# Convolution stage of a hybrid kernel: half of the Toeplitz tiles loaded by DMA instead of built by transposes

## The chip, the cores and the metric

One core of a Trainium2 chip. The metric is the device time of one execution of the whole kernel in microseconds (us), lower is better. A fair part of the document is about four engines that work side by side: TensorE (PE; its weight loads are listed as PEld), VectorE (DVE), ScalarE (ACT) and GpSimd (POOL), and about SyncE (SP), which issues most of the loads from DRAM.

## The reference, cut to what matters

```python
# x: (16, 32, 16, 16) f32
def _L0_conv_ref(x, weight_comp, kpe):          # weight_comp (32, 169), kpe (1, 1, 51, 51)
    ...
    weight = weight_comp[:, IDX_MAP].reshape(dim, 1, KS, KS) + kpe      # KS = 51
    pad = KS // 2
    return jax.lax.conv_general_dilated(x, weight, window_strides=(1, 1), padding=[(pad, pad), (pad, pad)],
                                        dimension_numbers=('NCHW', 'OIHW', 'NCHW'), feature_group_count=dim)
```

It is a depthwise convolution: every channel has its own 51x51 filter, which is a coarse per-channel filter (weight_comp, its 169 values spread over the taps) plus one fine filter of positions that all channels share (kpe). An image is 16x16, so only the middle 31x31 taps meet it. The convolution's result is divided by its standard deviation per image and channel and added to x; behind it come a layer norm over channels, an attention over 256 tokens with a mask of spikes, and steps of attention and feed-forward layers that are chosen from the data. All of that is untouched by the change.

## The kernel before, in words

The convolution is done as matmuls with Toeplitz tiles: `toep[:, c, e, x]` has, for channel c, 128 rows (8 image rows of 16 columns) by 24 x 16 f32 (NE = 24, HW = 16); all 32 channels lie in the tile `big`, 128 x 12288 f32. A group of the convolution (cg, eight of them, CG = 8) is four channels; `convolve(j)` (L678) does the groups 2j and 2j + 1 with 32 matmuls.

The tiles are built per block of eight channels (ck = 0 to 3, C8 = 8). `filter_rows` (L374) adds the per-channel weights `wx` and the shared `kx` into `filt` with nine small additions: block 0 on VectorE, blocks 1 to 3 on POOL (L489). `toeplitz(ck)` (L662) transposes windows of `filt` on TensorE, 24 transposes (L675) into six PSUM banks; ACT (L1147) and VectorE (L1403) copy the banks into `big`, by the letters of TOEP (L301), three each for a block in blocks 1 to 3 (four and two in block 0).

The order of TensorE's work is written by hand (L709 to L734): toeplitz 0, means, toeplitz 1, convolve 0, sums of squares (L720), toeplitz 2, a small matmul for the variance (L726), convolve 1, toeplitz 3, to_tokens 0, convolve 2, to_tokens 1, convolve 3, to_tokens 2 and 3. `to_tokens` (L698) transposes scaled groups back (L704), four transposes each. The scaling by the reciprocal deviation is done by ACT (L1153) and VectorE (L1409), four groups each by the letters CDRAIN (L295). On VectorE's queue there stand, behind the copies: the reciprocal (L1424), scalings, the preparations L1433 to L1442 (block-diagonal weights, constants), the step table L1445 to L1453, the last scaling, and then the layer norm, which starts with L1498 (x plus convolution). The step table goes out by two small DMAs (L420, L422).

The loads are issued in this order (sizes in MB of 10^6 bytes): identity 0.066, wx of block 0 0.074, wx of blocks 1 to 3 0.221, xrev 0.524 (x, columns reversed, read by the convolution), constf 0.190, two of attention weights 0.035 and 0.021, xin 0.524 (x as it is, read at L1498), the step masks 0.001, maskc 0.262, gather 0.131, chosen 0.033, spread 0.016, all by SP; kx 0.254 by ACT at the start.

```python
TOEP = "AADADA" + "ADAADA" + "ADADAD" + "ADADAD"
CDRAIN = "AADDADAD"
for ck in (1, 2, 3):                                       # POOL
    filter_rows(ck, pool, nc.gpsimd.tensor_tensor, s_filtP)
```

Of the kernel before, what the change touches and what calls it, by code (L numbers as in the profile page):

```python
# [11 lines left out]
ALU = mybir.AluOpType  # L12
ACT = mybir.ActivationFunctionType
AX = mybir.AxisListType

P = 128
B, C, HW = 16, 32, 16
# [11 lines left out]
C8 = 8  # L29
NCK = C // C8  # L30
NB = 2 * HW - 1
NOPS, NSTEPS, HID = 19, 33, 128
# [5 lines left out]
NONE = 4 * NSTEPS  # L38
CG = C // GB
NV = 8  # L40
# [54 lines left out]
def build(nc, d):  # L95
    with ExitStack() as ctx:
        def sb(name, shape, dt=F32):
            return ctx.enter_context(nc.sbuf_tensor(name, shape, dt))

        def sem(name):  # L100
            return ctx.enter_context(nc.semaphore(name))
# [6 lines left out]
        def part(t, n):  # L108
# [19 lines left out]
        sqc = sb("sqc", [P, C, NH, B])  # L128
        wx = sb("wx", [P, NCK, NQ, HW])
        filt = sb("filt", [P, NCK, NB, HW])  # L130
        big = sb("big", [P, C * NE * HW])
# [112 lines left out]
            "deviation_ready", "rstd_ready"))  # L244
        s_conv, s_convA, s_convD = sem("conv_in_psum"), sem("conv_scaled_by_act"), sem("conv_scaled_by_dve")
        s_lnc, s_lns, s_lnv, s_lnd, s_ln = (sem(n) for n in (
# [44 lines left out]
        NT = NE // 4  # L291
        TBANK = [(0, 1, 5, 7, 6)[n % 5] for n in range(3 * NT)] + [(0, 1, 5, 7)[n % 4] for n in range(NT)]
        STATS = 4
        CBANK = (2, 2, 3, 3, 2, 3, 0, 1)
        CDRAIN = "AADDADAD"  # L295
        TOKENS = (4, 6)
# [3 lines left out]
        WARM = 20  # L300
        TOEP = "AADADA" + "ADAADA" + "ADADAD" + "ADADAD"  # L301
        CONVT = "DD"
# [26 lines left out]
        def count(who, owners):  # L329
            return sum(o == who for o in owners)  # L330
# [71 lines left out]
        def _(sp):  # L402
# [3 lines left out]
            sp.dma_start(flat(xrev[:, :, :, :]).rearrange("p (h n) -> p h n", h=NH),  # L406
                         d["xrev"].rearrange("(h p) n -> p h n", p=P)).then_inc(s_xrev, 16)
            sp.dma_start(constf[:, :], d["constf"]).then_inc(s_cf, 16)
            sp.dma_start(wl1[:, :], d["wl1"]).then_inc(s_wl1, 16)
            sp.dma_start(wl2[:, :], d["wl2"]).then_inc(s_wl2, 16)  # L410
            sp.dma_start(flat(xin[:, :, :, :]).rearrange("p (h n) -> p h n", h=NH),
                         d["xtok"].rearrange("(h p) n -> p h n", p=P)).then_inc(s_xin, 16)
            sp.dma_start(masks8[:, :, :], d["masks"]).then_inc(s_tabl, 16)
            sp.dma_start(flat(maskc[:, :, :]), d["maskc"]).then_inc(s_mask, 16)
# [65 lines left out]
        def _(pool):  # L480
# [7 lines left out]

            for ck in (1, 2, 3):  # L489
                filter_rows(ck, pool, nc.gpsimd.tensor_tensor, s_filtP)  # L490
# [153 lines left out]
        def _(pe):  # L644
# [17 lines left out]
            def toeplitz(ck):  # L662
                for i in range(NT):
                    n = ck * NT + i
                    done = 1 + group_of(4 * i + 3 + YH - 1 - 15)
                    if ck == 0:
                        pe.wait_ge(s_filtD, done)
                    else:
                        pe.wait_ge(s_filtP, NQ * (ck - 1) + done)
                    if TBANK[n] in TBANK[:n]:  # L670
                        last = max(m for m in range(n) if TBANK[m] == TBANK[n])
                        pe.wait_ge(s_toepA if TOEP[last] == "A" else s_toepD, count(TOEP[last], TOEP[:last + 1]))
                    for u in range(4):
                        a0 = 4 * i + 3 - u
                        mm = pe.transpose(bank[TBANK[n]][:, u * P:(u + 1) * P], flat(filt[:, ck, a0:a0 + YH, :]), ident)  # L675
                    mm.then_inc(s_toep, 1)

            def convolve(j):  # L678

                for who, s in (("A", s_toepA), ("D", s_toepD)):  # L680
                    pe.wait_ge(s, count(who, TOEP[:(j + 1) * NT]))
                if j == 2:
                    for who, s in (("A", s_convA), ("D", s_convD)):
                        pe.wait_ge(s, count(who, CDRAIN[:4]))
# [12 lines left out]

            def to_tokens(j):  # L698

                for who, s in (("A", s_convA), ("D", s_convD)):  # L700
                    wait(pe, s, 0, count(who, CDRAIN[:2 * j + 2]))
# [428 lines left out]
        def _(act):  # L1130
# [18 lines left out]
            def scale_conv(j):  # L1149
                act.wait_ge(s_conv, j + 1)  # L1150
                for cg in (2 * j, 2 * j + 1):
                    if CDRAIN[cg] == "A":
                        nc.scalar.activation(convr[:, cg, :], bank[CBANK[cg]][:, (cg % 2) * S:(cg % 2 + 1) * S], ACT.Copy,  # L1153
                                             scale=rstd[:, cg:cg + 1]).then_inc(s_convA, 1)

# [232 lines left out]
        def _(dve):  # L1388
# [15 lines left out]

            def scale_conv(j):
                dve.wait_ge(s_conv, j + 1)
                for cg in (2 * j, 2 * j + 1):
                    if CDRAIN[cg] == "D":
                        nc.vector.tensor_scalar(convr[:, cg, :], bank[CBANK[cg]][:, (cg % 2) * S:(cg % 2 + 1) * S],  # L1409
                                                rstd[:, cg:cg + 1], None, ALU.mult).then_inc(s_convD, 1)  # L1410

# [9 lines left out]
            copy_toep(1)  # L1421
            copy_toep(2)
# [30 lines left out]
            nc.vector.tensor_copy(tabi[:, :], tabf[:, :]).then_inc(s_tabi, 1)  # L1453
            scale_conv(3)

# [414 lines left out]
```

## Time and profile before

| What | us |
|---|---|
| median of 3 runs | 169.78 (167.17 to 170.43) |
| the profiled execution, its own time | 170.36 |
| its span, first to last instruction | 168.5 |
| TensorE busy | 149.9 (89%) |
| VectorE busy | 110.8 (66%) |
| ACT busy | 76.0 (45%) |
| POOL busy | 60.1 (36%) |
| mean TensorE clock granted | 0.954 of full speed |

The span is what the hardware profiler saw between the first and the last instruction; 1.86 us of the execution's own time lie around it. Every row of the trace is placed in the span. Busy TensorE counts a matmul until its modelled end, so neighbouring matmuls overlap and a busy engine need not be at its peak. A row's duration is that of one instruction or of a merged group (x24 means 24 of them); two that follow one another on VectorE or ACT overlap a little, so the distance from start to start is less than the duration. "<-" with a name behind a row in brackets gives the idle time before it and what ended it.

### The profile page before, as it was taken

The numbers are of one execution on the slowest core, as the hardware profiler recorded it, in microseconds if no ns is written. First come the engines' busy times: TensorE is split into PE (matmuls) and PEld (weight loads), VectorE is DVE, ScalarE is ACT, GpSimd is POOL, SyncE is SP. The second block draws the span as 40 slices with busy tenths as digits, with TensorE's granted clock in tenths as the row PEclk, the third lists the DMA queues.
The fourth block names the chain that finished last, engine by engine and source line by source line (L and its number), as shares of the span: only waits on it lengthen the run. The fifth ranks groups of instructions, "written<-read, shape, count | busy, mean of one in ns | idle before, by whom it ended". The sixth has DMA issues, their size and how long they took to land.

```text
span 168.5 us, 4445 instructions
## 1 busy us (share of the span) xinstructions
PE 149.9 (89%) x1483; PEld 93.0 (55%) x1484; DVE 110.8 (66%) x362; ACT 76.0 (45%) x156; POOL 60.1 (36%) x160
## 2 busy tenths in 40 slices
PE   7999999779997879999887978999999799999942
PEld 5977784326483546464544336856654387666310
DVE  0561577894897559857741826659986735998862
ACT  3354642043757434244642524745444657343630
POOL 2494000004001778650230005786800268864000
PEclk9999999999999999999995589999999999999985
DMA  4920000000000000000100100000010000000012
GB/s 150 312 97 4 0 4 0 3 0 4 2 0 0 4 4 0 0 4 0 33 0 2 35 0 0 0 4 0 6 31 0 4 0 0 0 0 0 0 62 72
DMA packets 3023, 3.53 MB, mean 21 GB/s; under 512 B 505, under 2 KB 2361, under 8 KB 3002
## 3 DMA queue, kind: packets, MB, share of 16 engines
q1 hardware_dynamic: 2858, 3.00, 5.8%
q8 instruction: 12, 0.20, 0.5%
q10 hardware_dynamic: 144, 0.25, 0.4%
q14 instruction: 9, 0.07, 0.2%
HBM read 2.73 MB, written 0.53 MB: 19 GB/s over the span
## 4 chain that ended last, share of the span: by engine, by line
PE 60%; DVE 19%; POOL 7%; issue 7%; ACT 3%; DVEq 1%; ACTq 1%; POOLq 0%
PE bank L608 9%; PE bank L590 7%; POOL shifted L474 7%; PE bank L675 7%; PE bank L930 5%; DVE shifted L1589 4%; PE bank L904 4%; PE bank L913 3%; PE bank L693 3%; PE bank L924 3%; PE bank L660 3%; DVE sinv L1687 2%; DVE sinv L1596 2%; PE bank L573 2%; PE bank L886 1%
## 5 line engine op out<-in xcount | busy, mean ns | idle before, releaser
L474 POOL TENSOR_SCALAR shifted<-shifted,nmax 128x256 f32<-128x256 f32 x96 | 44.2, 478 | 44.9 <-DVE nmax L1589 44.9
L1127 ACT ACTIVATE big<-bank 128x512 f32<-128x512 f32 x48 | 27.4, 596 | 30.9 <-PE bank L608 30.5
L608 PE MATMUL bank<-ident,shifted 128*128 128x128 f32 x192 | 28.5, 281 | 4.3 <-POOL shifted L474 3.9
L1589 DVE CUSTOM_DVE_ANT_0 shifted<-bank,zeros 128x256 f32<-128x256 f32 x64 | 22.7, 420 | 13.0 <-PE bank L590 12.8
L608 PEld LDWEIGHTS bank<-ident,shifted 128*128 128x128 f32 x192 | 20.7, 141 | 13.3 <-POOL shifted L474 9.7
L1687 DVE RECIPROCAL sinv<-bank 128x256 f32<-128x256 f32 x8 | 14.1, 1758 | 2.0 <-PE bank L913 1.8
L1589 DVE CUSTOM_DVE_ANT_0 shifted<-bank,negm 128x256 f32<-128x256 f32 x32 | 11.3, 421 | 4.4 <-PE bank L590 4.3
L1279 ACT ACTIVATE big<-bank,wfs 128x512 f32<-128x512 f32 x14 | 8.8, 684 | 7.0 <-PE bank L924 7.0
L1147 ACT ACTIVATE big<-bank 128x512 f32<-128x512 f32 x14 | 8.2, 598 | 8.5 <-PE bank L675 8.5
L675 PEld LDWEIGHTS bank<-ident,filt 128*128 128x128 f32 x96 | 11.1, 147 | 1.0 <-issue 0.7
L675 PE MATMUL bank<-ident,filt 128*128 128x128 f32 x96 | 11.6, 279 | 0.0
L1403 DVE COPY big<-bank 128x512 f32<-128x512 f32 x10 | 6.8, 687 | 6.9 <-PE bank L675 6.8
L930 PE MATMUL bank<-big,wfs 128*32 128x256 f32 x96 | 8.8, 510 | 1.8 <-DVE big L1697 1.5
L590 PE MATMUL bank<-hT,qT 32*128 32x256 f32 x128 | 9.2, 400 | 1.0 <-ACT qT L1267 1.0
L655 PE MATMUL bank<-constf,ident 128*128 128x512 bf16 x35 | 9.4, 381 | 0.7 <-DVE xc L1480 0.6
L924 PE MATMUL bank<-hT,wfs 32*128 32x512 f32 x48 | 9.4, 804 | 0.6 <-DVE hT L1690 0.6
L381 POOL TENSOR_TENSOR filt<-kx,wx 128x16 f32<-128x16 f32 (+3 forms) x27 | 7.1, 314 | 4.9 <-DMA wx<-wx_dram 4.9
L503 POOL TENSOR_TENSOR bdv<-wvo,constf 128x128 f32<-128x128 f32 x1 | 0.5, 457 | 23.3 <-ACT bvo L1177 23.3
L913 PE MATMUL bank<-big,onesc 128*32 128x256 f32 x128 | 8.5, 384 | 0.0
L904 PE MATMUL bank<-big,v 128*32 128x256 f32 x128 | 8.5, 384 | 0.0
L1596 DVE RECIPROCAL sinv<-bank 128x256 f32<-128x256 f32 x4 | 7.0, 1756 | 2.0 <-PE bank L626 2.0
L1589 DVE DVE_READ_ACCUMULATOR2_ANT nmax<- 128x1 f32 x96 | 8.0, 83 | 0.0
(194 smaller groups left out, 228.8 us busy)
## 6 DMA issues: line engine op xcount, KB each, us to landing
xrev<-xrev_dram SPq DMA_DIRECT2D x1, 512.0 KB, 5.6
xin<-xtok_dram SPq DMA_DIRECT2D x1, 512.0 KB, 5.7
out_dram<-outT SPq DMA_DIRECT2D x2, 256.0 KB, 2.2
maskc<-maskc_dram SPq DMA_DIRECT2D x1, 256.0 KB, 5.5
kx<-kx_dram ACTq DMA_DIRECT2D x1, 248.0 KB, 3.1
wf<-wf_dram SPq DMA_DIRECT2D x3, 81.0 KB, 1.9
wx<-wx_dram SPq DMA_DIRECT2D x1, 216.0 KB, 4.8
constf<-constf_dram SPq DMA_DIRECT2D x1, 186.0 KB, 5.6
```

Of the source, the lines that this page charges most:

```text
L474: last = nc.gpsimd.tensor_scalar(sh[b % NSH][:, ih, :], sh[b % NSH][:, ih, :], -1.0, nmax[:, b, ih:ih + 1], ALU.mult, ALU.add)
L590: mm = pe.matmul(bank[b % 4][:, h * S:(h + 1) * S], qT[rows, g, h * P:(h + 1) * P], keys[rows, g, :], start=True, stop=True, tile_position ...
L608: mm = pe.transpose(bank[4 + b % 2][:, jh * S + ih * P:jh * S + (ih + 1) * P], sh[b % NSH][:, ih, jh * P:(jh + 1) * P], ident)
L675: mm = pe.transpose(bank[TBANK[n]][:, u * P:(u + 1) * P], flat(filt[:, ck, a0:a0 + YH, :]), ident)
L904: mm = pe.matmul(WEIGHED[g][q * C:(q + 1) * C, 0:S], v[:, jh, b, :], probT[b][:, jh, :], start=(jh == 0), stop=(jh == NH - 1), tile_positi ...
L913: mm = pe.matmul(out[q * C:(q + 1) * C, S:2 * S], onesc[:, :], probT[g * GB + q][:, jh, :], start=(jh == 0), stop=(jh == NH - 1), tile_pos ...
L924: pe.matmul(bank[banks[q]][:, 0:n], w1r[rows, :], flat(hT[rows, gs[0]:gs[0] + len(gs), :]), start=True, stop=True, tile_position=(q * C, 0 ...
L930: mm = pe.matmul(bank[into][q * C:(q + 1) * C, 0:S], w2s, relu[:, q, g, :], start=True, stop=True, tile_position=(0, q * C))
L1127: nc.scalar.activation(flat(probT[b]), bank[4 + b % 2][:, :], ACT.Exp).then_inc(s_P, 1)
L1589: m = nc.vector.tensor_tensor_reduce(sh[b % NSH][:, ih, :], scores[:, ih * S:(ih + 1) * S], negm[:, ih, :] if masked else zeros[:, :], -1. ...
L1596: link(nc.vector.reciprocal(sinv[:, g, :], bank[YBANKS[g % 2]][:, S:2 * S]))
L1687: nc.vector.reciprocal(sinv[:, g, :], SUMS[g][:, S:2 * S]).then_inc(s_inv, 1)
```

## The change

The tiles of channels 16 to 31 (groups 4 to 7) are no longer built on the chip. The per-channel part of each lies expanded in DRAM (`tw`) and is loaded straight into its place in `big`, one load of 128 x 1536 f32 per group; the shared part, also expanded (`tk`, 128 x 384), is loaded once into `taps`, and VectorE adds it in place to each group (`add_taps`). Toeplitz blocks 2 and 3, their filter additions on POOL and their copies are gone; `wx` and `filt` shrink to two blocks. TensorE's order becomes: toeplitz 0, means, toeplitz 1, convolve 0, sums of squares, convolve 1 (the variance matmul ahead of its last group), convolve 2, to_tokens 0, convolve 3, to_tokens 1, 2, 3. A convolution counts its semaphore up after each group, and groups 4 to 7 each wait for their addition. All eight scalings are ACT's. VectorE's queue behind the copies of block 1: additions for groups 4 and 5, L1433 to L1442, the reciprocal, additions for groups 6 and 7, the step table, the layer norm. SP's order: xrev, taps, groups 4 and 5, constf, attention weights, step masks, groups 6 and 7, xin, maskc and the rest.

```diff
+NCT = NCK // 2
+LC = NCT * C8 // GB
...
+        taps = sb("taps", [P, NE * HW])
...
-        CBANK = (2, 2, 3, 3, 2, 3, 0, 1)
-        CDRAIN = "AADDADAD"
+        CBANK = (2, 2, 3, 3, 0, 1, 2, 3)
...
-        TOEP = "AADADA" + "ADAADA" + "ADADAD" + "ADADAD"
+        TOEP = "AADADA" + "ADAADA"
...
+            def filters_of(cg):
+                n = GB * NE * HW
+                sp.dma_start(big[:, cg * n:(cg + 1) * n], d["tw"][:, (cg - LC) * n:(cg - LC + 1) * n]).then_inc(s_tw[cg - LC], 16)
+
+            sp.dma_start(taps[:, :], d["tk"]).then_inc(s_taps, 16)
+            filters_of(LC)
+            filters_of(LC + 1)
             sp.dma_start(constf[:, :], d["constf"]).then_inc(s_cf, 16)
             sp.dma_start(wl1[:, :], d["wl1"]).then_inc(s_wl1, 16)
             sp.dma_start(wl2[:, :], d["wl2"]).then_inc(s_wl2, 16)
+            sp.dma_start(masks8[:, :, :], d["masks"]).then_inc(s_tabl, 16)
+            filters_of(LC + 2)
+            filters_of(LC + 3)
             sp.dma_start(flat(xin[:, :, :, :]).rearrange("p (h n) -> p h n", h=NH),
                          d["xtok"].rearrange("(h p) n -> p h n", p=P)).then_inc(s_xin, 16)
...
-            for ck in (1, 2, 3):
+            for ck in (1,):
                 filter_rows(ck, pool, nc.gpsimd.tensor_tensor, s_filtP)
...
             def convolve(j):
...
+                if j < NCT:
+                    for who, s in (("A", s_toepA), ("D", s_toepD)):
+                        pe.wait_ge(s, count(who, TOEP[:(j + 1) * NT]))
+                if j == 3:
+                    pe.wait_ge(s_convA, 4)
                 for cg in (2 * j, 2 * j + 1):
+                    if cg == 3:
+                        pe.wait_ge(s_vhs, 1)
+                        pe.wait_ge(s_cf, 16)
+                        pe.matmul(bank[STATS][:, CG:2 * CG], pairs, vhalf[:, :], start=True, stop=True).then_inc(s_vp, 1)
+                    if cg >= LC:
+                        pe.wait_ge(s_filtered, cg - LC + 1)
...
-                mm.then_inc(s_conv, 1)
+                    mm.then_inc(s_conv, 1)
...
-            toeplitz(2)
-            pe.wait_ge(s_vhs, 1)
-            pe.wait_ge(s_cf, 16)
-            pe.matmul(bank[STATS][:, CG:2 * CG], pairs, vhalf[:, :], start=True, stop=True).then_inc(s_vp, 1)
             convolve(1)
-            toeplitz(3)
+            convolve(2)
             to_tokens(0)
-            convolve(2)
+            convolve(3)
             to_tokens(1)
-            convolve(3)
             to_tokens(2)
             to_tokens(3)
...
+            def scale_conv(cg):
+                act.wait_ge(s_conv, cg + 2 if cg in (0, 2) else cg + 1)
+                nc.scalar.activation(convr[:, cg, :], bank[CBANK[cg]][:, (cg % 2) * S:(cg % 2 + 1) * S], ACT.Copy,
+                                     scale=rstd[:, cg:cg + 1]).then_inc(s_convA, 1)
...
-            scale_conv(0)
-            copy_toep(3)
-            scale_conv(2)
-            scale_conv(3)
+            for cg in range(CG):
+                scale_conv(cg)
...
+            def add_taps(cg):
+                n = GB * NE * HW
+                rows = big[:, cg * n:(cg + 1) * n].rearrange("p (c n) -> p c n", c=GB)
+                dve.wait_ge(s_tw[cg - LC], 16)
+                nc.vector.tensor_tensor(rows, rows, rep(taps[:, :], GB), ALU.add).then_inc(s_filtered, 1)
...
             copy_toep(1)
-            copy_toep(2)
-            dve.wait_ge(s_std, 1)
-            nc.vector.reciprocal(rstd[:, :], stdv[:, :]).then_inc(s_rstd, 1)
-            dve.wait_ge(s_rstd, 1)
-            scale_conv(1)
-            copy_toep(3)
-            scale_conv(2)
+            dve.wait_ge(s_taps, 16)
+            add_taps(LC)
+            add_taps(LC + 1)
...
             nc.vector.memset(dec[0][:, :], DECAY)
+            dve.wait_ge(s_std, 1)
+            nc.vector.reciprocal(rstd[:, :], stdv[:, :]).then_inc(s_rstd, 1)
+            add_taps(LC + 2)
+            add_taps(LC + 3)
```

## Rows read from the trace of the kernel before

**Rows 1.** The page: busy time, and the granted clock in 40 slices
```profile
PE 149.9 (89%) x1483; PEld 93.0 (55%) x1484; DVE 110.8 (66%) x362; ACT 76.0 (45%) x156; POOL 60.1 (36%) x160
...
PEclk9999999999999999999995589999999999999985
```

**Rows 2.** The chain that ended last, 10 to 32 us: start, us, piece
```profile
14.67 1.88 PE bank L720 x16
16.55 2.68 PE bank L675 x24
19.22 0.12 PE bank L726 x2
19.35 1.86 PE bank L693 x32
21.21 2.77 PE bank L675 x24
23.98 0.44 PE bank L704 x4
...
30.00 0.40 DVE convr L1409
...
31.06 0.70 DVE tok L1498
```

**Rows 3.** Timeline by engine: start, us, instruction
```profile
12.16 1.27 DVE L1403 COPY big<-bank 128x512 f32<-128x512 f32 x2
...
26.75 0.28 DVE L1433 SCALAR_TENSOR_TENSOR centre<-constf,ident 128x128 f32<-128x128 f32 x1
...
28.41 0.18 DVE L1446 CAST maskf<-masks 19x66 f32<-19x66 uint8 x1
...
17.08 0.60 ACT L1147 ACTIVATE big<-bank 128x512 f32<-128x512 f32 x1 [0.32 <-PE bank L675]
...
20.10 0.84 ACT L1153 ACTIVATE convr<-bank,rstd 128x256 f32<-128x256 f32 x2 [0.44 <-DVE rstd L1424]
...
30.54 0.63 PE L704 MATMUL bank<-ident,convr 128*128 128x128 f32 x4 [1.22 <-DVE convr L1409]
...
4.20 0.43 SPq L411 DMA_DIRECT2D xin<-xtok_dram  x1
```

**Rows 4.** VectorE's additions by line: duration ns min/median/max, starts, forms
```profile
L1604 DVE TENSOR_TENSOR outT<-outT,yn x2: 424/424/425, 77.3 to 82.4; 128x256 f32<-128x256 f32 x2
...
L1480 DVE TENSOR_TENSOR xc<-tok,mu x2: 692/692/693, 32.7 to 35.0; 128x512 f32<-128x512 f32 x2
...
L1419 DVE TENSOR_TENSOR xcc<-xrev,bank x2: 1087/1092/1096, 10.3 to 11.2; 128x512 f32<-128x512 f32 x2
```

**Rows 5.** Stretches, us: busy PE PEld DVE ACT POOL; PEclk, DMA share, GB/s
```profile
0.00:6.00 6.00, 4.96 (x24) 3.79 (x26) 1.31 (x11) 1.50 (x3) 1.11 (x12) 1.00 0.61 188
4.00:5.00 1.00, 1.00 (x6) 0.74 (x5) 0.87 (x8) 0.00 (x0) 0.00 (x0) 1.00 0.91 219
5.00:9.00 4.00, 4.00 (x29) 3.63 (x28) 1.74 (x5) 2.18 (x4) 2.47 (x10) 1.00 1.01 343
```

**Rows 6.** Load of xin: KB, us from issue to landing
```profile
xin<-xtok_dram SPq DMA_DIRECT2D x1, 512.0 KB, 5.7
```

**Rows 7.** Stretches around the fall of the clock, columns as in rows 5
```profile
87.00:88.00 1.00, 0.73 (x3) 0.29 (x2) 0.75 (x2) 0.00 (x0) 0.00 (x0) 1.00 0.00 0
88.00:98.00 10.00, 8.73 (x55) 3.30 (x54) 4.46 (x11) 3.74 (x7) 0.09 (x1) 0.50 0.06 16
```

**Rows 8.** TensorE by form, 88 to 101 us, then 120 to 136
```profile
L924 PE MATMUL bank<-hT,wfs 32*128 32x512 f32 x16 | 4.9, 1133 | 0.0
L930 PE MATMUL bank<-big,wfs 128*32 128x256 f32 x32 | 3.6, 634 | 0.1
...
L924 PE MATMUL bank<-hT,wfs 32*128 32x512 f32 x16 | 2.3, 640 | 0.0
L930 PE MATMUL bank<-big,wfs 128*32 128x256 f32 x32 | 2.1, 385 | 0.0
```

More of the change, by code:

```diff
@@ L30 @@
 NCK = C // C8
+NCT = NCK // 2
+CG = C // GB
+LC = NCT * C8 // GB
 NB = 2 * HW - 1
@@ L38 @@
 NONE = 4 * NSTEPS
-CG = C // GB
 NV = 8
@@ L128, in build @@
         sqc = sb("sqc", [P, C, NH, B])
-        wx = sb("wx", [P, NCK, NQ, HW])
-        filt = sb("filt", [P, NCK, NB, HW])
+        wx = sb("wx", [P, NCT, NQ, HW])
+        filt = sb("filt", [P, NCT, NB, HW])
+        taps = sb("taps", [P, NE * HW])
         big = sb("big", [P, C * NE * HW])
@@ L244, in build @@
             "deviation_ready", "rstd_ready"))
-        s_conv, s_convA, s_convD = sem("conv_in_psum"), sem("conv_scaled_by_act"), sem("conv_scaled_by_dve")
+        s_conv, s_convA = sem("conv_in_psum"), sem("conv_scaled")
+        s_taps, s_filtered = sem("position_filter_loaded"), sem("position_filter_added")
+        s_tw = [sem(f"channel_filters_loaded{i}") for i in range(CG - LC)]
         s_lnc, s_lns, s_lnv, s_lnd, s_ln = (sem(n) for n in (
@@ L291, in build @@
         NT = NE // 4
-        TBANK = [(0, 1, 5, 7, 6)[n % 5] for n in range(3 * NT)] + [(0, 1, 5, 7)[n % 4] for n in range(NT)]
+        TBANK = [(0, 1, 5, 7, 6)[n % 5] for n in range(NCT * NT)]
         STATS = 4
-        CBANK = (2, 2, 3, 3, 2, 3, 0, 1)
-        CDRAIN = "AADDADAD"
+        CBANK = (2, 2, 3, 3, 0, 1, 2, 3)
         TOKENS = (4, 6)
@@ L410, in _ @@
             sp.dma_start(wl2[:, :], d["wl2"]).then_inc(s_wl2, 16)
+            sp.dma_start(masks8[:, :, :], d["masks"]).then_inc(s_tabl, 16)
+            filters_of(LC + 2)
+            filters_of(LC + 3)
             sp.dma_start(flat(xin[:, :, :, :]).rearrange("p (h n) -> p h n", h=NH),
                          d["xtok"].rearrange("(h p) n -> p h n", p=P)).then_inc(s_xin, 16)
-            sp.dma_start(masks8[:, :, :], d["masks"]).then_inc(s_tabl, 16)
             sp.dma_start(flat(maskc[:, :, :]), d["maskc"]).then_inc(s_mask, 16)
@@ L678, in convolve @@
             def convolve(j):
[L680 to L684, printed above, removed]
-                for cg in (2 * j, 2 * j + 1):
+                if j < NCT:
[3 more added lines that the diff above has]
+                    pe.wait_ge(s_convA, 4)
+                for cg in (2 * j, 2 * j + 1):
+                    if cg == 3:
[4 more added lines that the diff above has]
+                        pe.wait_ge(s_filtered, cg - LC + 1)
                     for hi in range(NH):
@@ L695, in convolve @@
                                            tile_position=(0, q * 32))
-                mm.then_inc(s_conv, 1)
+                    mm.then_inc(s_conv, 1)
             def to_tokens(j):
-                for who, s in (("A", s_convA), ("D", s_convD)):
-                    wait(pe, s, 0, count(who, CDRAIN[:2 * j + 2]))
+                pe.wait_ge(s_convA, 2 * j + 2)
                 for h in range(NH):
@@ L1147, in copy_toep @@
                         nc.scalar.activation(dst, src, ACT.Copy).then_inc(s_toepA, 1)
[L1149 to L1154, printed above, removed]
+            def scale_conv(cg):
+                act.wait_ge(s_conv, cg + 2 if cg in (0, 2) else cg + 1)
+                nc.scalar.activation(convr[:, cg, :], bank[CBANK[cg]][:, (cg % 2) * S:(cg % 2 + 1) * S], ACT.Copy,
+                                     scale=rstd[:, cg:cg + 1]).then_inc(s_convA, 1)
             act.wait_ge(s_zero, 2)
@@ L1403, in copy_toep @@
                         nc.vector.tensor_copy(dst, src).then_inc(s_toepD, 1)
[L1405 to L1410, printed above, removed]
+            def add_taps(cg):
[3 more added lines that the diff above has]
+                nc.vector.tensor_tensor(rows, rows, rep(taps[:, :], GB), ALU.add).then_inc(s_filtered, 1)
             nc.vector.memset(dmax[:, :], 0.0).then_inc(s_rD, 1)
@@ L1421, in _ @@
             copy_toep(1)
-            copy_toep(2)
-            dve.wait_ge(s_std, 1)
-            nc.vector.reciprocal(rstd[:, :], stdv[:, :]).then_inc(s_rstd, 1)
-            dve.wait_ge(s_rstd, 1)
-            scale_conv(1)
-            copy_toep(3)
-            scale_conv(2)
+            dve.wait_ge(s_taps, 16)
+            add_taps(LC)
+            add_taps(LC + 1)
             dve.wait_ge(s_cf, 16)
@@ L1453, in _ @@
             nc.vector.tensor_copy(tabi[:, :], tabf[:, :]).then_inc(s_tabi, 1)
-            scale_conv(3)
             def argmax_op(values, n):
@@ L1841 @@
     columns = _np.array([[group_of(HW - 1 - k) for k in line] for line in shifts])
+    reach = NE - 1 - _np.arange(NE) + _np.arange(YH)[:, None]
+    groups = _np.array([[group_of(k - HW + 1) for k in line] for line in reach])[:, :, None, None]
     kper = g["L0_conv_kpe"][0, 0, :, ::-1]
@@ L1847 @@
         "xtok": tok(g["x"]), "xrev": tok(g["x"][:, :, :, ::-1]),
-        "wx": wc[:, :, columns].reshape(NCK, C8, NQ, HW, HW).transpose(3, 1, 0, 2, 4).reshape(P, NCK * NQ * HW),
+        "wx": wc[:NCT * C8, :, columns].reshape(NCT, C8, NQ, HW, HW).transpose(3, 1, 0, 2, 4).reshape(P, NCT * NQ * HW),
+        "tw": wc[NCT * C8:, groups, columns].transpose(1, 4, 0, 2, 3).reshape(P, (C - NCT * C8) * NE * HW),
+        "tk": kper[R - HW + 1 + reach[:, :, None, None], R - HW + 1 + shifts].transpose(0, 3, 1, 2).reshape(P, NE * HW),
         "kx": _np.repeat(kper[R - HW + 1:R + HW, R - HW + 1 + shifts].transpose(1, 0, 2), C8, axis=0).reshape(P, NB * HW),
```

## The prediction

> **What bounds the kernel now.** I read the totals first [rows 1]: TensorE is busy for 89% of the span, but one share says little of a kernel with several stages, so the next view is the chain that ended last, in order of time, for the stretch the change touches [rows 2]. Until 26.3 us it runs through TensorE: transposes of filter rows (L675), convolution matmuls (L693), the sums of squares (L720), two transposes to token order (L704). Then it passes to VectorE, whose run of small preparations (L1433 at 26.75 to L1453 [rows 3]) stands ahead of the last scaled channel group (L1409, 30.00 [rows 2]); the last transposes follow, and at 31.06 the layer norm starts with L1498. So two things in one row set the start of the layer norm: TensorE's issue order, and VectorE's queue. The loads are no limit today: xin, the last large one that anything in this stretch reads, is issued at 4.20 [rows 3] and lands 5.7 later [rows 6], at 9.9, and is read at 31.06. What the change must be judged by is one number: when L1498 starts. What follows it (layer norm, projections, spike scan, attention, the steps) is untouched and hangs on it.
>
> **What goes.** Two of four blocks of transposes: 24 each, 2.68 and 2.77 us of the chain [rows 2], 5.45 us of TensorE. With them go twelve copies out of PSUM, six on ACT (0.60 each) and six on VectorE (two took 1.27) [rows 3], and 18 of POOL's 27 small additions, which only the transposes that go with them wait for. VectorE's four scalings go to ACT, which then has eight at 0.42 apiece in a row (a pair took 0.84 [rows 3]): 3.4 us.
>
> **What comes on VectorE.** Four additions in place over 128x1536 f32, both sources in SBUF. No row has this size. The nearest are L1604 at 424 ns for 256 elements (in place, too) and L1480 at 692 for 512 [rows 4]: 268 ns for the step from 256 to 512, so 1.05 ns an element; 1024 elements more than L1480 make 692 + 1072 = 1.76 us recorded. Neighbours overlap by about 0.08 (two copies of 0.69 recorded took 1.27 [rows 3]; four such additions overlap as little), so an addition takes 1.68 us of the queue. The other end is L1419, at 1087 to 1096 ns for 512 elements [rows 4]; less the same overlap, 1.01 us per 512: 3.03 us. I take 1.68, because L1419 writes with a long stride and the new one is contiguous, like L1480 and L1604; the lower end is the same 1.68, since nothing in the trace adds two f32 tensors at less than 1.05 ns an element.
>
> The Trainium skill (SBUF — State Buffer, Door 1, on cachelines) says that accesses which leave a 16-byte line each time pay for it and contiguous ones do not. By that rule L1419 is slow for its stride and the sum is mine; if instead two-input additions were slow for another reason, the sum would be that of the second rival below. No row here separates the two.
>
> **What comes on the DMA engines.** One load of 128x384 f32 (0.197 MB) and four of 128x1536 (0.786 MB each), 3.34 MB against 2.35 MB of loads before, while one wx load shrinks from 0.221 to 0.074 MB. I add up bytes in queue order. Before, 188 GB/s over the first 6.0 us are 1.13 MB moved, and from 5 to 9 us the rate was 343 GB/s [rows 5]. The landing that an engine can see lags the bytes: xin ends at 1.91 MB of the queue, reached at 6.0 + 0.78/0.343 = 8.3, and landed at 9.9 [rows 3, 6]. So I add 1.6 us. After the change xrev ends at 0.99 MB and the position filter at 1.19 MB, about 6.2 us. From there at 343 GB/s: first filter block (1.97 MB) lands at 10.1, second 12.4, constf 12.9, the small weights 13.1, third block 15.4, fourth 17.7, xin 19.2, maskc 20.0. SP issues four large loads more at 0.4 to 0.5 us each, all ahead of need. As bounds of the rate I take 219 GB/s, from 4 to 5 us the poorest microsecond once the loads run [rows 5] (fourth block 23.3), and no limit at all from above, since an earlier landing gains nothing. Instruction code comes through the same DMA engines; from 5 to 9 us, with DMA busy throughout, TensorE was busy for all of the four [rows 5], so I cost it at 0 and keep 1.6, one landing lag, as its upper end.
>
> **The new schedule.** Nothing up to 16.4 us changes: the first two transpose blocks, the first convolution and the sums of squares keep their places, ending at 16.55 (14.67 + 1.88 [rows 2]).
> VectorE: its last PSUM copy of block two ends its slot at 13.4 (12.16 + 1.27 [rows 3]). First addition to 15.1, second to 16.75. Then L1433 to L1442, 26.75 to 28.41 before [rows 3], 1.66 us: 18.4. The deviation is ready by then (TensorE's L726 lies inside the second convolution at about 17.5, ACT's root takes 0.27), so the reciprocal goes out at 18.4, done by 18.6. Third addition to 20.25, fourth to 21.95. Table preparations, 28.41 to 30.00 before [rows 2, 3], 1.55 us: 23.5.
> TensorE: convolution 1 with L726 from 16.5, 1.86 + 0.12, to 18.5. Convolution 2 needs additions one and two (15.1, 16.75): to 20.4. Tokens 0 (0.44 [rows 2]) to 20.85. Convolution 3 needs four scalings (18.6 + 4 x 0.42 = 20.3) and addition three (20.25): its first half to 21.8. Its second half waits for addition four, 22.0, and ends at 23.0. ACT scales the last group by 23.45 while TensorE does tokens 1 and 2 (0.44 each, to 23.9); tokens 3 starts there. L1498 came 0.52 after that point before (30.54 to 31.06 [rows 2, 3]), so now at 24.4. VectorE has been free since 23.5 and xin landed at 19.2.
> Gain: 31.06 - 24.4 = 6.66 us. TensorE and VectorE are within 0.2 us of one another at 21.8 to 22.0; what is late next is VectorE's queue, and every 0.1 us more per addition costs 0.4. The waits added are all VectorE's, for loads. Behind them stand in turn the second addition, L1433 to L1442, the reciprocal (ACT's eight scalings wait for it) and the table; covers are 3.3 us for the first block, 2.7 for the second, 3.1 for the third, 2.5 for the fourth (needed at 20.25). The last is gone below 272 GB/s: (4.58 - 1.19 MB) / (18.65 - 6.2 us). The step table's two small DMAs, come 6 us earlier and stay off the chain.
>
> **The sum.** The profiled execution took 170.36 us around a span of 168.5. 170.36 - 6.66 = 163.7. Its time lies 0.58 above the median of the three runs, 169.78; against the median 163.1, which I predict. A measurement of this kernel can tell about 2% from no change (the three runs lie 3.26 us apart).
>
> **The clock** widens the range most. The granted clock fell to 0.50 (1.2 GHz) from 88 to 98 us, after TensorE had been busy for 0.73 of the microsecond before [rows 7], with VectorE's and ACT's short group statistics in between. Inside that stretch 16 matmuls of L924 took 4.9 us and 32 of L930 took 3.6; at 2.4 GHz the same took 2.3 and 2.1 [rows 8]: about 4.1 us for one such stretch. The change leaves that place alone, so it should come again, 6.7 us earlier; but its length can differ between runs. The Trainium skill (TensorE: Matmul & The Clock Gate, Part 1) says that the gate's timing is independent of the kernel's start and differs from run to run. By that rule the 6.66 stands and only the spread grows; if the shift itself made a second stretch, 4.1 us of the gain would go.
>
> **The rivals.**
> 1. *The loads come too late, in part.* At 219 GB/s the fourth block's bytes end at 6.2 + 3.39/0.219 = 21.7 and land at 23.3. From there: addition 1.68, half a convolution 1.0, tokens 1 and 2 0.88, L1498's 0.52, together 4.1: start 27.4, gain 3.7, time 166.1. For it: 219 GB/s stands in the trace. Against: the four microseconds behind it at 343 [rows 5].
> 2. *VectorE becomes the bound.* At 3.03 us an addition: 13.4 + 6.06 + 1.66 + 0.15 + 6.06 = 27.35, and 1.0 + 0.88 + 0.52 more: 29.75, gain 1.3, time 168.5. For it: L1419. Against: every contiguous row.
> 3. *Slower than before: the filter loads take the place of the transposes.* The wait before the fourth addition becomes the bound. It cancels the whole gain when block four lands at 31.06 - 4.1 = 26.96, bytes done at 25.4, that is below 3.39/19.2 = 177 GB/s. At 160, less than half of 343, its bytes end at 6.2 + 3.39/0.16 = 27.4, it lands at 29.0 and L1498 starts at 33.1: 2.0 us slower, 171.8 against the median. For it: this is the one resource whose use more than doubles, and pieces of 6 KB a partition are a shape no row of the trace has. Against: no microsecond of the running loads was under 219.
> 4. *A second stretch at 1.2 GHz.* 163.1 + 4.1 = 167.2. For it: the trace has such a stretch, and another at the end, where it is cheap [rows 1]. Against: the idle time that comes before the fall is not made longer.
>
> **How the numbers follow.** Forecast 0.70; rival 1 0.11; rival 2 0.06; rival 3 0.04; rival 4 0.09. The time is the forecast's. The range goes down 2.6 us (the fastest run of before lies that far under its median): 160.5. Upwards it takes in rivals 1 and 4 and stops short of rival 2: 167.2. Faster by over 2% means under 166.4: the forecast, most of rival 1, a little of rival 4 together 0.83; within 2% 0.13, from rivals 1, 2, 4 and part of 3; slower 0.04, what rival 3 holds at still poorer rates and what I have not thought of.
>
> **What would show it.** Right: L675 with 48 matmuls, L1498's successor starting at 24 to 25 us; four additions of 1.7 to 1.8 us; TensorE waiting some tenths of a microsecond for the fourth; GB/s above 300 from 5 to 17 us; ACT with eight scalings. Wrong: VectorE idle until a DMA ends ahead of any addition (rival 1 or 3), additions of 3 us (rival 2), a gap on an engine while loads run that no semaphore explains (code), the layer norm 6 us earlier but the end not (rival 4, or a wait further on for something I took as free, such as maskc).

## The result, and the profile after

The kernel takes 163.46 us (median of 4 runs, 162.23 to 164.32) against 169.51 (4 runs): 0.968 of before, with a 95% interval of 0.962 to 0.973, so it is faster by 2.7 to 3.8%. The profiled execution took 164.04 us around a span of 162.3; before it was 170.36 and 168.5. The profiled executions differ by 6.3 us and the medians by 6.05, where 6.66 were forecast.

First the page, sections 1 and 2, of the kernel after:

```profile
PE 144.3 (89%) x1432; PEld 88.2 (54%) x1436; DVE 111.4 (69%) x356; ACT 74.2 (46%) x154; POOL 55.4 (34%) x142
...
PEclk9999999999999999999955699999999999999985
...
GB/s 112 303 402 417 138 4 1 0 2 0 6 0 2 2 0 4 0 4 31 0 6 0 31 0 4 0 4 2 10 27 0 4 0 0 0 0 0 0 65 75
```

Against [rows 1]: TensorE lost 5.6 us of busy time and still has 89% of a shorter span; VectorE is as busy as before, since four additions replaced six copies and four scalings. The loads stand in the first five slices of 4.06 us each, at 303 to 417 GB/s in slices 2 to 4.

Next the chain that ended last, 12 to 27 us (start, us, piece), to be laid beside [rows 2]:

```profile
13.06 1.86 PE bank L712 x32
...
18.11 2.73 PE bank L712 x48
20.84 0.59 PE bank L722 x4
21.43 1.86 PE bank L712 x32
23.29 1.26 PE bank L722 x10
...
24.64 0.70 DVE tok L1504
```

The two pieces of transposes are gone (L675 in [rows 2]) and so is VectorE's piece ahead of the last transposes; TensorE holds the chain from the first convolution (L712) to the last token transposes (L722) without a gap (three pieces, TensorE's too, are left out here). The layer norm starts at 24.64, at 31.06 before.

VectorE's and ACT's rows in the same stretch (timeline: start, us, instruction), and the four additions by line:

```profile
13.56 3.41 DVE L1417 TENSOR_TENSOR big<-big,taps 128x1536 f32<-128x1536 f32 x2
...
18.59 3.36 DVE L1417 TENSOR_TENSOR big<-big,taps 128x1536 f32<-128x1536 f32 x2
...
18.70 1.93 ACT L1164 ACTIVATE convr<-bank,rstd 128x256 f32<-128x256 f32 x5 [0.28 <-DVE rstd L1447]
```

```profile
L1417 DVE TENSOR_TENSOR big<-big,taps x4: 1687/1743/1753, 13.6 to 20.2; 128x1536 f32<-128x1536 f32 x4
```

Idle time ahead of an instruction stands in brackets, as behind L1164. None stands behind the additions: VectorE never waited for a load. The fourth ends at 21.95, and TensorE reaches its group at about 22.4.

The loads, in stretches of one us or more (last two columns: DMA share, GB/s), and xin's by landing:

```profile
0.00:6.00 6.00, 4.96 (x24) 3.79 (x26) 1.30 (x11) 1.50 (x3) 1.73 (x14) 1.00 0.52 134
5.00:9.00 4.00, 4.00 (x29) 3.70 (x28) 1.63 (x4) 2.04 (x4) 3.22 (x15) 1.00 0.97 367
...
12.00:13.00 1.00, 1.00 (x13) 0.83 (x11) 1.00 (x3) 0.87 (x2) 0.00 (x0) 1.00 1.05 436
...
15.00:16.00 1.00, 1.00 (x11) 1.00 (x11) 1.00 (x2) 0.00 (x0) 0.00 (x0) 1.00 1.00 395
...
17.00:18.00 1.00, 1.00 (x18) 0.48 (x10) 1.00 (x6) 0.01 (x1) 0.00 (x0) 1.00 0.73 244
```

```profile
xin<-xtok_dram SPq DMA_DIRECT2D x1, 512.0 KB, 10.7
```

Over the first six us the rate is lower than in [rows 5] (134 against 188 GB/s), from 5 to 9 us it is higher (367 against 343). Nearly all bytes are through by 18 us. The last block of filters landed 9.1 us after its issue at 7.1, at 16.2, and its addition started at 20.2.

**A better ruler than the start of the span.** In the profiled runs the convolutions do not start at one time: 12.74 us before, 12.99 after, 11.71 to 13.15 in the experiments. The same matmuls in the opening run at two speeds. TensorE by line from 6.2 to 6.8 us (busy us, mean ns, idle time), before and then after:

```profile
L675 PE MATMUL bank<-ident,filt 128*128 128x128 f32 x8 | 1.1, 283 | 0.0
```

```profile
L688 PE MATMUL bank<-ident,filt 128*128 128x128 f32 x5 | 1.1, 365 | 0.0
```

Up to about 6 us they take 421 ns and then 273; where that change comes earlier, all that follows does too. It came later in this profile than in that of before, and from the start of the span that hides 0.25 us of the gain: 31.06 - 24.64 is only 6.42. So I measure from the first convolution matmul to the first addition of the layer norm: **31.06 - 12.74 = 18.32 before, 24.64 - 12.99 = 11.65 after, 6.67 less**. I call this the stage. What follows it is unchanged: from the layer norm to the spike mask's sum (L1553 before, L1559 after) 20.82 us before and 20.83 after, and to the end of the span 137.4 and 137.7.

### The profile page after: what moved, and what is told of

Same layout as the page of the kernel before. It is cut to its first block, busy times and chain, and to the rows that moved or that the text cites. A ratio compares the mean times of both kernels' runs of the same rounds, so it can differ in the third digit from the quotient of the medians.

```text
span 162.3 us, 4306 instructions
## 1 busy us (share of the span) xinstructions
PE 144.3 (89%) x1432; PEld 88.2 (54%) x1436; DVE 111.4 (69%) x356; ACT 74.2 (46%) x154; POOL 55.4 (34%) x142
## 4 chain that ended last, share of the span: by engine, by line
PE 60%; DVE 18%; POOL 7%; issue 7%; ACT 3%; DVEq 2%; ACTq 1%; POOLq 0%
PE bank L621 10%; PE bank L603 8%; POOL shifted L487 7%; PE bank L943 5%; PE bank L712 5%; DVE shifted L1595 4%; PE bank L917 4%; PE bank L688 4%; PE bank L926 4%; PE bank L937 3%; PE bank L673 3%; DVE sinv L1693 2%; DVE sinv L1602 2%; PE bank L586 2%; PE bank L899 1%
## 5 line engine op out<-in xcount | busy, mean ns | idle before, releaser
L1140 ACT ACTIVATE big<-bank 128x512 f32<-128x512 f32 x48 | 27.4, 596 | 30.9 <-PE bank L621 30.5
L668 PE MATMUL bank<-constf,ident 128*128 128x512 bf16 x32 | 8.8, 381 | 1.1 <-DVE xc L1486 0.6
L1703 DVE TENSOR_SCALAR big<-bank,wfs 128x512 f32<-128x512 f32 x10 | 7.0, 744 | 1.2 <-PE bank L937 1.2
L712 PE MATMUL bank<-big,xcc 128*16 128x256 f32 (+1 forms) x128 | 7.7, 382 | 0.0
L1160 ACT ACTIVATE big<-bank 128x512 f32<-128x512 f32 x8 | 4.7, 598 | 6.3 <-PE bank L688 6.3
L603 PEld LDWEIGHTS bank<-hT,qT 32*128 32x128 f32 x128 | 5.8, 184 | 3.0 <-issue 2.0
L943 PEld LDWEIGHTS bank<-big,wfs 128*32 128x32 f32 x96 | 3.2, 135 | 7.5 <-DVE big L1703 4.3
## 6 DMA issues: line engine op xcount, KB each, us to landing
xin<-xtok_dram SPq DMA_DIRECT2D x1, 512.0 KB, 10.7
```

What stands on the lines that cost most here:

```text
L603: mm = pe.matmul(bank[b % 4][:, h * S:(h + 1) * S], qT[rows, g, h * P:(h + 1) * P], keys[rows, g, :], start=True, stop=True, tile_position ...
L943: mm = pe.matmul(bank[into][q * C:(q + 1) * C, 0:S], w2s, relu[:, q, g, :], start=True, stop=True, tile_position=(0, q * C))
L1140: nc.scalar.activation(flat(probT[b]), bank[4 + b % 2][:, :], ACT.Exp).then_inc(s_P, 1)
```

## The experiments

Theory: TensorE's written order sets the stage; the two blocks of transposes were 5.45 us of it and VectorE's place in the queue the rest; loads and additions lie beside it. Rivals: the order of the queues made the gain; VectorE, or the loads, are already the bound.

**1. Preparations first, in the kernel before.**

```diff
             copy_toep(3)
-            scale_conv(2)
-
             dve.wait_ge(s_cf, 16)
...
             nc.vector.memset(dec[0][:, :], DECAY)
+            scale_conv(2)
```

> The kernel before, with VectorE's preparations (L1433 to L1442) moved ahead of its scaling of group 4, so that only the step table stands ahead of the last scaling. Theory (TensorE's order is the bound and only 1.2 us of the 6.4 gained came from VectorE's queue): the last scaling goes out right behind the last convolution at 28.8 instead of 29.93, the layer norm starts at 29.8 instead of 31.06, and the time falls by 1.25 us. Rival (the gain of the change was mostly the better order of the queues, not the transposes that went): the layer norm starts before 28.5 and the time falls by 2.5 us or more.

Stage 29.03 - 11.81 = 17.22 us, 1.10 less than before. The chain of waits:

```profile
27.81 0.59 PE bank L704 x4
28.40 0.11 issue
...
29.03 0.70 DVE tok L1498
```

The last scaling goes out with the end of the convolution. The time is 168.42 us, 0.989 of before (0.985 to 0.992): 0.8 to 1.5% less, and the 1.25 us expected are 0.7%. By the time alone the run would not settle it: the medians differ by 2.15 us (170.57 to 168.42), and L1498 starts at 29.03 instead of 31.06, both nearer to the rival's figures than to the 1.25 of the theory. But 0.93 of these 2.03 us lie ahead of the first convolution (11.81 against 12.74), where the edit moves nothing and the speed of the opening's matmuls does. In the stage, the order of VectorE's queue is worth 1.10 us, a sixth of the change's gain, and there the rival falls.

**2. One more addition in the changed kernel.**

```diff
...
+            nc.vector.tensor_tensor(idle[:, :].rearrange("p (c n) -> p c n", c=GB), rep(taps[:, :], GB), rep(taps[:, :], GB), ALU.add)
             add_taps(LC + 2)
```

> The changed kernel with one more addition of the same size on VectorE, into a tile that nobody reads, ahead of the addition for group 6. Theory (TensorE's order is the bound and VectorE ends the fourth addition about 0.4 us ahead of need): the layer norm starts 1.68 - 0.4 = 1.3 us later, at 25.9. Rival A (VectorE is the bound already, as the prediction had it): 1.7 us later. Rival B (VectorE has wide cover): under 0.3 us.

Stage 25.07 - 11.96 = 13.11 us, 1.46 more than after. The chain changes sides:

```profile
17.65 1.62 DVE idle L1449
19.26 3.35 DVE big L1418 x2
...
22.66 1.07 PE bank L713 x16
```

The new addition took 1.62 us of the queue and cost 1.46: cover (the time by which an engine is done ahead of need) is small but there. TensorE now waited for VectorE twice, 0.68 and 0.51 us, ahead of groups 6 and 7. 1.46 lies between the 1.3 of the theory and the 1.7 of rival A, so this run alone doesn't part them; run 7 does. The time was 163.13 us (0.960 of before, 0.953 to 0.966), which by itself would show nothing: its profiled execution had a shorter stretch at 1.2 GHz (mean clock 0.970 against 0.952) and an early start. Only the stage is comparable.

**3. One block of transposes put back, without copies.**

```diff
             convolve(1)
+            for i in range(NT):
+                for u in range(4):
+                    a0 = 4 * i + 3 - u
+                    pe.transpose(bank[5][:, u * P:(u + 1) * P], flat(filt[:, 1, a0:a0 + YH, :]), ident)
             convolve(2)
```

> The changed kernel with 24 transposes put back between convolutions 1 and 2, into a bank that nobody reads, with no copies behind them. Theory: TensorE's order is the bound, so the whole 2.75 us comes back; the layer norm starts at 27.4 and the time rises to 166.2. Rival (the copies or the waits between transposes and copies were the cost, not TensorE's time): under 1 us.

The chain of waits:

```profile
18.84 2.77 PE bank L745 x24
```

It has the block in full. Stage 27.27 - 12.71 = 14.56 us, 2.91 more. Of these, 2.77 are the block; the rest is the convolution's matmuls falling into two pieces. The time is 166.58 us (0.978 of before, 0.971 to 0.985), 0.4 above the forecast. What the change saved is TensorE's time, not the copies.

**4. Three more loads.**

```diff
...
+            for i in range(3):
+                n = GB * NE * HW
+                sp.dma_start(idle[i][:, :], d["tw"][:, i * n:(i + 1) * n]).then_inc(s_idle, 16)
             filters_of(LC + 2)
```

> The changed kernel with three more loads of 0.786 MB, into tiles that nobody reads, ahead of the loads of groups 6 and 7. Theory (the loads are hidden; the fourth block lands at about 16.4 and is needed at 20.25, and the engines move 0.41 MB in a microsecond): 2.36 MB more delay it by 5.75 us to 22.15, past its cover, and the layer norm starts 1.5 us later, at 26.1. Rival A (the loads already set the time): 5 us or more later. Rival B (cover is wider, or the landing does not follow the bytes): no change.

Stage 26.80 - 13.15 = 13.65 us, 2.0 more. Timeline of VectorE, then the chain:

```profile
20.73 3.59 DVE L1422 TENSOR_TENSOR big<-big,taps 128x1536 f32<-128x1536 f32 x2 [1.87 <-DMA big<-tw_dram]
```

```profile
22.56 1.77 DVE big L1422
...
24.38 1.07 PE bank L717 x16
```

Now the bracket is there: VectorE waited 1.87 us for a load ahead of the third addition, and the fourth began when its own load had landed, at 22.56, where 22.15 was forecast. The last block landed 6.3 us later than in the changed kernel (22.54 against 16.2) and cost 2.0, where 1.5 was expected, so a little over 4 us lay under cover; the changed kernel's own trace has 4.0 between landing and addition (16.2 to 20.2). The time is 166.13 us, 0.978 of before (0.971 to 0.984). The rival in which the loads come too late begins at about 4 us of delay.

**5. The changed kernel again**, as the reference on the chip of runs 6 to 8.

> The changed kernel itself once more, on the chip of the three runs beside it, as their reference. Both theories: layer norm 11.65 us after the first convolution's start, as in its first profile (13.0 to 24.64); time about 0.967 of before.

Stage 24.32 - 12.66 = 11.66 us: the ruler repeats to 0.01. Time 162.68 us, 0.956 of before (0.951 to 0.962), where the first measurement had 0.968 (0.962 to 0.973): two measurements of one kernel whose intervals only touch. About 1% is thus what a ratio can tell here. The clock (stretches of two us, PEclk third from the end):

```profile
50.00:52.00 2.00, 2.00 (x18) 1.28 (x19) 0.39 (x3) 0.59 (x1) 1.08 (x3) 0.58 0.00 0
52.00:54.00 2.00, 2.00 (x12) 1.62 (x10) 2.00 (x13) 1.05 (x2) 1.51 (x4) 0.57 0.02 4
```

A second stretch at 1.2 GHz stands in the attention from 50 to 54 us, which neither first profile had; the known one, from about 81 us, ended at 88 instead of 92.

**6. Transposes to token order by half.**

```diff
-            to_tokens(0)
+            to_tokens(0, (0,))
             convolve(3)
-            to_tokens(1)
-            to_tokens(2)
-            to_tokens(3)
+            for h in range(NH):
+                for j in range(h == 0, CG // 2):
+                    to_tokens(j, (h,))
```

> The changed kernel with the transposes to token order sorted by half: those of the first half (which the first addition of the layer norm reads) of all groups first, those of the second half behind them. Theory (TensorE's order is the bound to its end): four transposes less stand ahead of the layer norm, but the last scaling ends at 23.83 and two transposes follow it, so it starts at 24.2 instead of 24.64, 11.2 us after the first convolution; 0.4 us of 163.5. Rival (the last scaling or VectorE's table is the bound): no change.

The end of the chain of waits, ahead of the layer norm:

```profile
21.83 0.59 PE bank L722 x4
22.42 0.01 issue
22.43 0.45 PE bank L722 x2
```

Stage 22.97 - 11.71 = 11.26 us, 0.40 less, as the theory had it. Its count was off: on the chain stand eight transposes instead of fourteen between convolution 2 and the layer norm, six less and not four. The time, 162.75 us and 0.962 (0.957 to 0.967) beside run 5's 0.956, can't show 0.4 us. The stage is shorter; a faster kernel is not shown.

**7. No additions.**

```diff
-                nc.vector.tensor_tensor(rows, rows, rep(taps[:, :], GB), ALU.add).then_inc(s_filtered, 1)
+                nc.vector.tensor_tensor(rows[:, 0, 0:1], rows[:, 0, 0:1], taps[:, 0:1], ALU.add).then_inc(s_filtered, 1)
```

> The changed kernel with the four additions cut to one element each: channels 16 to 31 are convolved without the filter of positions, the output differs. Theory (TensorE's order is the bound and the additions end ahead of need): the layer norm still starts 11.65 us after the first convolution, within 0.1, and the time stays. Rival (VectorE binds, as the prediction had it): 0.3 us or more earlier.

Stage 24.64 - 12.97 = 11.67 us: nothing moved. VectorE's wait ahead of the layer norm grew instead (timeline):

```profile
24.64 0.69 DVE L1504 TENSOR_TENSOR tok<-xin,bank 128x512 f32<-128x512 f32 x1 [4.38 <-PE bank L722]
```

It was 1.16 us with the additions. Four additions of 1.68 us are free here, all of them beside TensorE. The whole run took 191.15 us, with other data behind the stage; why it is longer there stays open, and only the stage is read.

**8. A quarter loaded** (channels 24 to 31; the third block of transposes, its POOL additions and copies back).

```diff
-NCT = NCK // 2
+NCT = 3
...
-TOEP = "AADADA" + "ADAADA"
+TOEP = "AADADA" + "ADAADA" + "ADADAD"
...
+            toeplitz(2)
             convolve(1)
...
             add_taps(LC)
-            add_taps(LC + 1)
+            copy_toep(2)
...
-            add_taps(LC + 2)
-            add_taps(LC + 3)
+            add_taps(LC + 1)
```

> Only channels 24 to 31 are loaded, channels 0 to 23 are built with transposes: two loads and two additions instead of four. Theory: one block of transposes is back in TensorE's order, 2.75 us, and nothing else binds; layer norm 14.4 us after the first convolution, time 166.2. Rival (half of the gain came from the order of VectorE's queue and the scalings on ACT, which this version keeps): under 1.5 us more than the changed kernel.

Stage 26.11 - 11.77 = 14.34 us, 2.69 more than after; time 165.24 us, 0.975 of before (0.968 to 0.981), 2.56 above run 5. Together with run 1 the account closes: 1.10 (queue) + 2.69 (this block) leaves 6.67 - 3.79 = 2.88 for the other, whose piece in [rows 2] is 2.68. The last figure is a remainder; no run takes that block out alone.

**9. Three quarters loaded.**

```diff
-NCT = NCK // 2
+NCT = 1
...
-            toeplitz(1)
...
-            copy_toep(1)
             dve.wait_ge(s_taps, 16)
-            add_taps(LC)
-            add_taps(LC + 1)
+            for cg in range(LC, LC + 4):
+                add_taps(cg)
...
-            add_taps(LC + 2)
-            add_taps(LC + 3)
+            add_taps(LC + 4)
+            add_taps(LC + 5)
```

> Only channels 0 to 7 are built with transposes, groups 2 to 7 are loaded: six loads and six additions on VectorE. The second block of transposes (2.62 us) ran beside VectorE's centring of x, on which the first convolution waits anyway, so it gives back at most 0.5 us of TensorE's order. Theory (VectorE takes over as the bound): 12.4 + 4 x 1.68 + 1.66 + 0.15 + 2 x 1.68 = 24.3 for the last addition, the layer norm at 26.8 where the changed kernel has 24.64, 18.2 us after the start of the means against 16.1 there, and 2.1 us more in all. Rival (what is loaded is gained, as half was): the layer norm 0.5 us or more earlier than in the changed kernel.

From the start of the means 26.60 - 7.66 = 18.94 us; after, 24.64 - 8.55 = 16.09. That is later, as the theory said, but 0.7 us more than its 18.2, and for another reason. The time is 165.96 us, 0.978 of before (0.968 to 0.987). The chain:

```profile
11.59 3.60 PE bank L709 x32
...
18.38 4.41 PE bank L709 x48
```

TensorE still holds it: the last addition ended at 23.1, ahead of need. But 32 convolution matmuls took 3.60 us instead of 1.86, and 48 took 4.41 instead of 2.73. In the stretches the granted clock (third from the end) fell twice:

```profile
9.00:11.00 2.00, 0.54 (x2) 0.00 (x0) 1.35 (x2) 0.00 (x0) 0.00 (x0) 1.00 1.01 418
11.00:13.00 2.00, 1.41 (x16) 0.67 (x20) 2.00 (x2) 1.15 (x2) 0.00 (x0) 0.65 1.01 424
13.00:15.00 2.00, 2.00 (x24) 0.60 (x16) 2.00 (x3) 0.00 (x0) 0.00 (x0) 0.50 1.06 407
15.00:17.00 2.00, 2.00 (x21) 1.87 (x18) 2.00 (x2) 0.00 (x0) 0.00 (x0) 1.00 1.01 414
17.00:19.00 2.00, 2.00 (x27) 1.03 (x30) 2.00 (x7) 0.45 (x2) 0.00 (x0) 0.86 1.00 398
19.00:21.00 2.00, 2.00 (x24) 1.01 (x20) 2.00 (x5) 1.14 (x4) 0.00 (x0) 0.50 0.86 321
```

TensorE was busy for 0.54 of the two us that the transposes had filled, and the granted clock fell to 0.50, which is 1.2 GHz. It fell a second time at about 18.5 us, though TensorE is listed as busy throughout from 13 us on, and that fall lengthened the 48 matmuls; what brought it on is not shown.

**10. Two of the six additions on POOL.**

```diff
+            for cg in (4, 5):
...
+                pool.wait_ge(s_tw[cg - LC], 16)
+                nc.gpsimd.tensor_tensor(rows, rows, rep(taps[:, :], GB), ALU.add).then_inc(s_filteredP, 1)
```

> As the run before it, with the additions of groups 4 and 5 on POOL, which is idle then. POOL's additions took 0.47 us for 128 elements and 0.73 for 256, so 3.3 us for 1536. Theory A (the two engines add beside one another): the second of POOL's ends at about 20.5, 1 us after TensorE wants it, and the layer norm starts 16.8 us after the start of the means, 0.7 us later than in the changed kernel. Theory B (two additions with both inputs in SBUF exclude one another on the two engines): all six take turns, 13.4 us from 12.4 on, and the layer norm starts about 19.5 us after the start of the means.

28.71 - 7.63 = 21.08 us; time 167.58 us, 0.988 of before (0.984 to 0.992). VectorE's timeline, then POOL's:

```profile
11.36 6.64 DVE L1422 TENSOR_TENSOR big<-big,taps 128x1536 f32<-128x1536 f32 x2
17.91 3.52 DVE L1440 SCALAR_TENSOR_TENSOR centre<-constf,ident 128x128 f32<-128x128 f32 x1
```

```profile
12.81 8.48 POOL L511 TENSOR_TENSOR big<-big,taps 128x1536 f32<-128x1536 f32 x2 [10.65 <-DMA big<-tw_dram]
```

Two additions took VectorE 6.64 us, 3.41 in the changed kernel, and the small L1440 took 3.52 us instead of 0.28 and was done when POOL was. POOL's own two took 3.56 and 4.96 us, where 3.3 was the estimate. Theory B holds: the two engines took turns. It was dearer than the 19.5 us expected, and both falls of the clock of run 9 are in it, too; how much each adds was not parted. The Trainium skill (SBUF — State Buffer, Who interferes with whom) has this as a rule: a VectorE instruction with two SBUF inputs contends with a GpSimd instruction that reads SBUF. The trace agrees, with 4.98 us for one of the two additions, where the shortest of the run took 1.69.

**11. Run 9 with TensorE kept busy.**

```diff
             mm.then_inc(s_mean, 1)
+            for i in range(20):
+                pe.matmul(bank[3][:, 0:2 * P], ones256[:, 0:P // 2].bitcast(BF16), ones256[:, :].bitcast(BF16), start=True, stop=True)
             pe.wait_ge(s_xc, NH)
```

> The kernel of e9 with twenty bf16 matmuls into a bank that nobody reads, between the means and the first convolution, where the second block of transposes had stood. In e9 TensorE waited 2.04 us there for the centring of x, and from 11.6 us on ran at 1.2 GHz: the first convolution took 3.60 us instead of 1.86. Theory (the transposes had kept the clock up, at no cost): the clock stays at 2.4 GHz, the convolution takes 1.86 us again, and VectorE becomes the bound as e9 was to show; the layer norm starts 17.9 us after the start of the means, against 18.9 in e9 and 16.1 in the changed kernel. Rival (the fall had nothing to do with the idle time): convolution 3.6 us, layer norm at 18.9 or later.

25.31 - 7.34 = 17.97 us, forecast 17.9. The stretch that had been at half clock, then the chain:

```profile
11.00:13.00 2.00, 2.00 (x36) 1.00 (x34) 2.00 (x3) 1.15 (x2) 0.00 (x0) 1.00 1.03 430
```

```profile
19.55 3.30 DVE big L1414 x2
...
22.89 1.07 PE bank L709 x16
```

The clock stays at 1.00, the second fall of run 9 is gone as well, and now VectorE is the bound. Useless matmuls gave 0.97 us back. The layer norm still comes 1.9 us later than in the changed kernel, and the chain there runs through VectorE's six additions instead of four. In the stage, half the channels is the best of the three splits that I ran. The time is 164.45 us, 0.968 of before (0.960 to 0.976), which does not part it from the changed kernel's 0.956 and 0.968. Not every wait brings the clock down: later in this run TensorE was busy for only 0.72 of two us, and the clock stayed at 1.00 there and up to 29 us:

```profile
19.00:21.00 2.00, 0.72 (x8) 0.42 (x4) 2.00 (x4) 1.42 (x4) 0.00 (x0) 1.00 0.85 317
```

## Why the prediction was right, point by point

- *What bounds.* TensorE's order and VectorE's queue: right. Runs 3 and 8 give 2.91 and 2.69 us for a block of transposes, charged at 2.68 and 2.77; run 1 gives 1.10 for the queue, for which the prediction's working left 6.66 - 5.45 = 1.2.
- *The additions.* Forecast were 1.68 us of the queue each: two took 3.41 together, one 1687 to 1753 ns against 1760 forecast. The overlap of 0.08 was right (two of 1.743 in 3.41), though the copies it was taken from give 2 x 0.69 - 1.27 = 0.11. L1419's rate, the upper end, was wrong for a contiguous operand. The Trainium skill's rule on cachelines (SBUF — State Buffer, Door 1), by which contiguous operands are not slowed, agrees; that L1419's stride is what slows it remains untested.
- *The loads.* Hidden: right, but two terms were mis-sized, in opposite directions. The rate was 367 GB/s from 5 to 9 us and 395 to 436 from 11 to 17, not 343, while the first six us moved 134 GB/s instead of 188. The fourth block landed at 16.2 (forecast 17.7), xin at 7.54 + 10.7 = 18.2 (forecast 19.2). Both errors fell on the cover, which was 4.0 us for the fourth block where 2.5 were given.
- *The schedule.* Layer norm at 24.64, forecast 24.4. The stage shrank by 6.67 us, forecast 6.66; the missing 0.25 is the later rise of the matmuls' speed in the opening, which the prediction did not have. That the stage agrees to 0.01 is luck in part: errors of 0.1 to 0.3 us cancel. "TensorE waiting some tenths of a microsecond for the fourth" addition did not happen. Measured from the first convolution, TensorE came to that group 0.3 later than forecast (the variance matmul took 0.32 of the chain instead of 0.12, the first tokens 0.59 instead of 0.44), VectorE was done 0.25 earlier, so the wait of 0.2 became 0, and what follows took 0.1 less. The order of the two was thus the other way round: TensorE is the bound, with VectorE 0.4 ahead of it, and run 7 shows that no part of the additions counts.
- *The rivals.* The sum of the second comes to 27.33 and not 27.35, which changes nothing. Loads too late: begins at about 4 us of delay (run 4). VectorE the bound: begins at one addition more (run 2) and holds with two more (run 11). Slower than before by the loads: even run 4, with 2.36 MB more, is not. A second stretch at 1.2 GHz: not in the profile after, but in run 5 of the same kernel, so it comes and goes with the execution. Five profiles have it in the attention (runs 5 to 9, run 7 on other data), all of the changed kernel or a variant of it, and neither of the two of the kernel before and its variant (run 1) does; whether the change makes it likelier is not shown.

## What to carry to other kernels

Work that filled a wait of TensorE cost nothing here, and taking it away did cost: the two blocks of transposes on the chain gave 5.6 us. The one beside VectorE's centring gave nothing: with it gone the layer norm came 2.85 us later, of which filling the wait again gave 0.97 back, and VectorE's two more additions set the rest. Ask of each block whether it stands in the chain or beside a wait, before moving it to DMA. Where a time moves by as much as its clock does from run to run, measure a stage between two instructions of one trace, and prove cover by using it up: one addition more, three loads more.

## What the runs showed of the hardware that I had not expected

- Loads of 0.786 MB in pieces of 6 KB a partition ran at 395 to 436 GB/s for six us (11 to 17), with TensorE and VectorE busy throughout and a convolution of 32 matmuls taking 1.86 us, as before; the loads of before had reached 343 over four us and 371 in the best one.
- Two us with TensorE busy for 0.54 in all were followed by 1.2 GHz at 11.6 us and a convolution twice as long (run 9); with twenty matmuls in that wait there was no fall (run 11). The second fall of run 9, at about 18.5 us, came with TensorE listed as busy throughout, and in run 11 two us with 0.72 busy were followed by none; neither is explained.
- VectorE and POOL adding side by side, all inputs in SBUF (run 10): 4.98 us for an addition that takes 1.69 alone, and a 0.28 us instruction drawn out to 3.52.
- The granted clock stands at 1.00 in the opening although the same transposes take 421 ns up to about 6 us and 273 ns behind; the moment of the change differed by a microsecond between profiled runs and moved everything behind it.
